# Softmax attention rebuilt: fp32r parts in two row tiles, wider exponentials, direct maxima

## The chip, the cores and the metric

The kernel runs on 1 core of one Trainium2 chip. The metric is the device time of one execution in microseconds. TensorE (PE) multiplies, VectorE (DVE), ScalarE (ACT) and GpSimd (POOL) work on elements, SyncE (SP) issues most DMAs. A difference of 0.2% is about what a measurement of this kernel can tell from none.

## What is computed

4096 tokens of 256 numbers pass a linear attention with exponential features, a layer norm, a transformer block, and a layer norm. The block is softmax attention with 16 heads of 16 numbers and a mixture of 8 experts, two per token. The part at issue, from the reference (the sequence is one batch of 4096):

```python
h = _layernorm(x, ln1_g, ln1_b)
q = (h @ Wq).reshape(Bb, Ss, H, Dh)
k = (h @ Wk).reshape(Bb, Ss, H, Dh)
v = (h @ Wv).reshape(Bb, Ss, H, Dh)
scores = jnp.einsum('bqhd,bkhd->bhqk', q, k) / jnp.sqrt(jnp.float32(Dh))
attn = jax.nn.softmax(scores, axis=-1)
ctx = jnp.einsum('bhqk,bkhd->bqhd', attn, v).reshape(Bb, Ss, Dd)
x = x + ctx @ Wo
```

Scores are large (Wq and Wk are scaled by 8), so q, k and the probabilities are carried in several parts of lower precision that add up to nearly fp32.

## The kernel before

The program runs its stages one after the other: linear attention with the projections (`linear_attention`), `softmax_attention`, `output_projection`, routing, dispatch, experts, combine.

In the last part of `linear_attention` each of eight chunks of 512 tokens is normalized (L407), transposed (L262), projected (L270, L276) and split into three bf16 parts: ScalarE writes the high one (L325), VectorE the rest (L423), ScalarE its middle (L331), VectorE the low one (L435). SyncE stores q, k and kd (the difference of the two halves of each 512 keys) to DRAM (L186, L190).

`softmax_attention` goes over 16 heads x 8 chunks of 512 queries; a chunk is a *step* of 16 units `t` of 256 keys (STEPS, STEP). Six products of parts stack up to 96 rows (SROWS); two more rows carry minus the maximum of each query (MROWS). In each unit TensorE does, in this order: `scores(t, 0)` (L683), `diff_unit` (L627), `scores(t, 1)`, `b_unit` (L636), `values` (L666) of five units ago (LAG). ScalarE turns scores into probabilities, two exponentials of 512 columns (L741), with the relu of `diff_unit` between them (L728). The maximum of each query over all keys is needed before the exponentials, so it is found seven steps ahead: for 1024 keys a unit computes b, the scores of one half, and diff, those of the other half minus b; max(b + relu(diff)) is made by one fused VectorE operation (`unit`, L797). diff_ps and b_ps have two buffers each. At the end of a step the tile maxima are reduced (L789), turned by TensorE (L642), split in two (L773, L775) and sent by SyncE into rows of q_ring (`rows`, L534). Probabilities are fp32; their upper 16 bits are read in place as bf16, and the low part is subtracted, by VectorE for 11 units (L804) and by GpSimd for 5 (L590). `values` multiplies both with V in three bf16 parts, as two column tiles side by side (partitions 0 to 63 and 64 to 127 of o_ps). Once a step ScalarE copies O (L733), TensorE turns it (L649), VectorE divides it (L781, L783) into ctx_slots. Before the first step stand seven steps of maxima only; in the last eight there are none.

The order on each engine is the order of the code; semaphores tie the engines together. `output_projection` gathers the heads (L880), turns them (L897), multiplies with Wo (L904) and adds x (L916) for each of eight chunks.

## Time and profile before

| | |
|---|---|
| median of 3 runs | 4858.36 us (4850.29 to 4861.54) |
| span of the profiled execution | 4852.0 us |
| PE, DVE, ACT, POOL busy | 4267.5, 3937.8, 3726.1, 2088.2 us |
| PE weight loads (overlap PE) | 1709.2 us |
| DMA | 176.11 MB, mean 36 GB/s |

The page's span goes from the first to the last instruction; it lies 6 us under the median. A busy share is an average over stages with different limits, so a change in one stage is read from that stage. Idle time of an engine is put down to the instruction that released it. TensorE's matmuls are pipelined: a row's duration reaches from its start to its last result, and the distance between two starts is what one costs in a stream.

### The profile page before, as it was taken

The page shows a single profiled execution, that of the slowest core. Times are in us where ns is not written, and L with a number is a line of the kernel's source. Part 1 is how long each engine was busy: PE and PEld are TensorE (multiplying, and loading weights), DVE is VectorE, ACT ScalarE, POOL GpSimd, SP SyncE. Part 2 cuts the span into 40 slices and gives each one's busy share as a digit, 9 for nine tenths or more (in the row PEclk, how much of TensorE's full clock was granted, in tenths as well). Part 3 has the DMA queues.
Part 4 walks back from the last instruction along what each step waited for, and adds up shares of the span by engine and source line. Part 5 has one row for each costly group of instructions (what it writes and reads, how often), then busy time and mean ns, then how long its engine had stood idle before and what let it go on. Part 6 is the DMA issues. An engine that isn't in the chain of part 4 may idle for free. (4 is left out here: it accounts for less than half of the span.)

```text
span 4852.0 us, 96386 instructions
## 1 busy us (share of the span) xinstructions
PE 4267.5 (88%) x22137; PEld 1709.2 (35%) x22137; DVE 3937.8 (81%) x7272; ACT 3726.1 (77%) x6966; POOL 2088.2 (43%) x1034
## 2 busy tenths in 40 slices
PE   7569999999999999999999999999999860899991
PEld 4322222222222222222222222222222350788881
DVE  3558898889899888989988898989998651788875
ACT  1347999999999999999999999999999720454440
POOL 0011343434444343434434343434434405787775
PEclk8777999999999999999999999999999965899995
DMA  2231010100101010100101010110100032333323
GB/s 77 100 81 17 0 17 0 17 6 11 17 0 17 0 17 0 17 11 6 16 0 17 0 17 0 17 16 0 17 0 1 37 104 88 134 122 121 124 98 112
DMA packets 105459, 176.11 MB, mean 36 GB/s; under 512 B 16512, under 2 KB 87552, under 8 KB 99072
## 3 DMA queue, kind: packets, MB, share of 16 engines
q1 hardware_dynamic: 86864, 146.17, 11.7%
q0 software_dynamic: 6336, 16.79, 1.1%
q10 hardware_dynamic: 12144, 12.06, 0.7%
q14 instruction: 97, 0.79, 0.1%
q8 instruction: 18, 0.29, 0.0%
HBM read 117.55 MB, written 57.15 MB: 36 GB/s over the span
## 5 line engine op out<-in xcount | busy, mean ns | idle before, releaser
L741 ACT ACTIVATE probs<-s_ps 128x512 f32<-128x512 f32 x4096 | 2427.4, 600 | 213.7 <-PE s_ps L683 160.9
L590 POOL TENSOR_TENSOR probs_low<-probs 128x1024 f16<-128x1024 f32 x640 | 1324.9, 2071 | 2082.7 <-ACT probs L741 2082.2
L804 DVE TENSOR_TENSOR probs_low<-probs 128x1024 f16<-128x1024 f32 x1408 | 1820.3, 1295 | 20.8 <-ACT probs L741 20.7
L797 DVE CUSTOM_DVE_ANT_0 excess<-b_ps,excess 128x512 f32<-128x512 f32 x2048 | 1402.1, 687 | 333.3 <-ACT excess L728 265.4
L683 PE MATMUL s_ps<-q_ring,k_ring 98*128 (+1 forms) x4096 | 1565.0, 384 | 14.4 <-ACT probs L741 9.3
L728 ACT ACTIVATE excess<-diff_ps 128x512 f32<-128x512 f32 x2048 | 1214.5, 593 | 58.2 <-PE diff_ps L627 48.2
L666 PE MATMUL o_ps<-probs,v_parts 128*64 128x512 bf16 x4106 | 853.9, 412 | 74.5 <-ACT o_here L733 72.2
L627 PE MATMUL diff_ps<-kd_ring,q_ring 96*128 (+1 forms) x2048 | 800.6, 391 | 50.8 <-issue 38.3
L683 PEld LDWEIGHTS s_ps<-q_ring,k_ring 98*128 98x128 bf16 x4096 | 434.8, 106 | 1159.8 <-ACT probs L741 572.4
L636 PE MATMUL b_ps<-k_ring,q_ring 96*128 (+1 forms) x2048 | 797.9, 390 | 12.5 <-DVE unit_max L797 11.9
L666 PE MATMUL o_ps<-probs_low,v_parts 128*64 128x512 f16 x4106 | 783.7, 378 | 0.0
L666 PEld LDWEIGHTS o_ps<-probs,v_parts 128*64 128x64 bf16 x4106 | 228.3, 106 | 907.8 <-issue 511.3
L1506 DVE TENSOR_TENSOR hidden_low<-hidden,hidden_high 128x512 fp32r<-128x512 f32 x184 | 436.6, 2397 | 123.1 <-ACT hidden_high L1470 122.8
L1466 ACT ACTIVATE hidden<-h_ps,b_here 128x512 f32<-128x512 f32 x184 | 127.1, 691 | 306.0 <-PE h_ps L1401 285.6
L1413 PE MATMUL y_ps<-w_high,hidden_high 128*128 128x256 f32 x736 | 213.4, 290 | 41.4 <-DVE hidden_low L1506 41.3
L636 PEld LDWEIGHTS b_ps<-k_ring,q_ring 96*128 (+1 forms) x2048 | 200.5, 98 | 128.2 <-DVE unit_max L797 61.3
L627 PEld LDWEIGHTS diff_ps<-kd_ring,q_ring 96*128 (+1 forms) x2048 | 201.4, 98 | 99.0 <-issue 93.1
L666 PEld LDWEIGHTS o_ps<-probs_low,v_parts 128*64 128x64 bf16 x4106 | 233.6, 109 | 0.3
L649 PEld LDWEIGHTS misc_ps<-gather,o_here 128*128 128x128 f32 x1032 | 153.2, 188 | 216.5 <-issue 215.3
L1413 PE MATMUL y_ps<-w_low,hidden_high 128*128 128x256 f32 x736 | 211.9, 288 | 0.0
L1413 PE MATMUL y_ps<-w_high,hidden_low 128*128 128x256 f32 x736 | 210.6, 286 | 0.0
L649 PE MATMUL misc_ps<-gather,o_here 128*128 128x17 f32 x1032 | 203.6, 273 | 0.7 <-ACT o_here L733 0.7
(199 smaller groups left out, 3521.3 us busy)
## 6 DMA issues: line engine op xcount, KB each, us to landing
w_in<-in_W SPq DMA_DIRECT2D x46, 1024.0 KB, 4.9
q_ring<-qs_dram SPq DMA_DIRECT2D x96, 128.0 KB, 4.4
k_ring<-ks_dram SPq DMA_DIRECT2D x96, 128.0 KB, 7.2
slots_dram<-zero_rows SPq DMA_DIRECT2D x24, 512.0 KB, 6.5
rows_e<-slots_dram SPq DMA_DIRECT2D x24, 512.0 KB, 3.9
y_slots_dram<-y_out ACTq DMA_DIRECT2D x23, 512.0 KB, 4.6
...
```

Source lines behind the costliest of these rows:

```text
L590: nc.gpsimd.tensor_tensor(probs_low[:, t % BUFS, :, :], probs[:, t % BUFS, :, :], high[:, :, :, 1], ALU.subtract).then_inc(pool_low_done, 1)
L627: nc.tensor.matmul(diff_ps[:, u % 2, :], q_ring[0:SROWS, ds(q, P)], kd_ring[:, ds(k, CHUNK)], start=True, stop=True).then_inc(diff_done, 1)
L636: nc.tensor.matmul(b_ps[:, u % 2, :], q_ring[0:SROWS, ds(q, P)], keys[:, :, 1, :], start=True, stop=True).then_inc(b_done, 1)
L649: last = nc.tensor.matmul(out_ps[:, t, :], o_here[:, P * t:P * t + P], gather[:, :], start=True, stop=True)
L666: last = nc.tensor.matmul(o_ps[V_COLS * k:V_COLS * k + V_COLS, :], v_parts[:, par, 2 * at + k, :], part[:, k, :], start=(t == 0 and low == ...
L683: nc.tensor.matmul(s2_ps[:, k, :], k_ring[:, col:col + P], q, start=True, stop=True).then_inc(s2_done, 1)
L728: nc.scalar.activation(excess[:, u % 2, :], diff_ps[:, u % 2, :], ACT.Relu).then_inc(excess_ready, 1)
L741: nc.scalar.activation(probs[:, t % BUFS, k, :], s2_ps[:, k, :], ACT.Exp).then_inc(exp_done, 1)
L797: nc.vector.tensor_tensor_reduce(excess[:, u % 2, :], b_ps[:, u % 2, :], excess[:, u % 2, :], 1.0, LEAST, ALU.add, ALU.max, unit_max[:, u ...
L804: nc.vector.tensor_tensor(probs_low[:, t % BUFS, :, :], probs[:, t % BUFS, :, :], high[:, :, :, 1], ALU.subtract).then_inc(low_done, 1)
L1413: last = nc.tensor.matmul(y_ps[:, b, t // 2, D * (t % 2):D * (t % 2) + D], h[:, f % 4, cols], w[:, b, f, :], start=(f == 0 and n == 0 and ...
L1506: nc.vector.tensor_tensor(hidden_low[:, f % 4, :], hidden[:, f % 2, :], hidden_high[:, f % 4, :].bitcast(F32), ALU.subtract).then_inc(low_ ...
```

## The change

Projections: q, k and kd are split into two fp32r parts instead of three bf16 ones, so ScalarE's middle parts and VectorE's low parts go. The stores are 8 a chunk instead of 6, of 8 bytes an element instead of 6.

Attention: three products of parts take 48 rows, so the scores of two key tiles are two row tiles, at partitions 0 and 64, and q is loaded to both places (q_stage, a chunk at a time, three ahead). One exponential takes both results, 1024 columns. The maximum is found two chunks ahead (LEAD) in 16 pairs of 512-column matmuls a chunk, in three banks of PSUM: in 11 pairs VectorE reduces both banks directly, in 5 (RELU_PAIRS) the old form with kd and a relu by ScalarE stays. The tile maxima are turned by VectorE in blocks of 32 and sent by 16 small DMAs. P times V: in 4 of 16 units (FULL_UNITS) P and V are multiplied in plain fp32, in 12 P is high and low as before; GpSimd makes the low parts of ten units, VectorE those of two, in four halves (DVE_PLACES). `values` come in ten visits, up to a slot in the next chunk (SLOTS). O is turned by one fp32 matmul of 512 columns (gather now 128 x 128), copied by ScalarE and stored undivided in DRAM with its sums. `output_projection` loads these, takes 1/z, spreads it over the heads with a matmul of ones, and VectorE multiplies; TensorE's transposes of heads and ScalarE's copies go, GpSimd adds x1 and x2. The division per chunk and ctx_slots go.

Longer functions are cut; lines taken away stand only where they are short.

```diff
-PARTS = 3
...
-Q_PARTS = (0, 0, 0, 1, 1, 2)
-K_PARTS = (0, 1, 2, 0, 1, 0)
...
+PARTS = 2
+Q_PARTS = (0, 0, 1)
+K_PARTS = (0, 1, 0)
...
+FULL_UNITS = (3, 7, 11, 15)
+DVE_UNITS = (2, 10)
+POOL_UNITS = (0, 1, 4, 5, 6, 8, 9, 12, 13, 14)
...
+DVE_PLACES = {5: (2, 0), 8: (2, 1), 11: (10, 0), 14: (10, 1)}
+VISITS = ((0, 1), (3,), (2, 4), (7,), (5, 6), (8, 9), (11,), (10, 12), (15,), (13, 14))
+SLOTS = (11, 12, 13, 14, 15, 16, 17, 18, 19, 21)
+COPY_SLOT, TURN_SLOT = 6, 8
+RELU_PAIRS = (2, 5, 8, 11, 14)
+FINISH_SLOTS = (4, 5, 6, 7)
+M_BANKS = tuple(((t + 1) % 3, t % 3 if t < UNITS - 1 else 2) for t in range(UNITS))
...
-                for s in range(5):
-                    act.wait_ge(rest_ready, c * 5 + (s + 6))
-                    nc.scalar.activation(parts[:, b, s, 1, :], rest[:, s, :], ACT.Copy).then_inc(mid_ready, 1)
...
-                for s in range(5):
-                    dve.wait_ge(mid_ready, c * 5 + (s + 1))
-                    nc.vector.tensor_tensor(parts[:, b, s, 2, :], rest[:, s, :], parts[:, b, s, 1, :], ALU.subtract
-                                            ).then_inc(low_ready, 1)
...
+        s_ps = ps("s_ps", [P, 2, 2, CHUNK])
+        m_ps = ps("m_ps", [P, 3, CHUNK])
...
+            def rows(n, buf):
+                sp.wait_ge(max_ready, n + 1)
+                for at in (0, TOP_ROW):
+                    for r in range(MROWS):
+                        row = q_stage[at + SROWS + r:at + SROWS + r + 1, ds(buf * CHUNK, CHUNK)].bitcast(F32)
+                        row = row.rearrange("a (t b n) -> a t b n", t=TPC, b=P // SQ)
+                        for b in range(P // SQ):
+                            sp.dma_start(row[:, :, b, :], max_turned[SQ * b:SQ * b + TPC, r, :]).then_inc(rows_in, 16)
...
+                for t in POOL_UNITS:
+                    pool.wait_ge(exp_done, i * UNITS + (t + 1))
+                    nc.gpsimd.tensor_tensor(probs_low[:, LOW_UNITS.index(t), :, :], probs[:, t, :, :],
+                                            high_view[:, t, :, :, 1], ALU.subtract).then_inc(pool_low_done, 1)
...
+            def max_pair(it, c, t):
+                g = it * (PAIR * UNITS) + (c * UNITS + t)
+                par, buf = c % PAIR // CHUNKS, c % Q_BUFS
+                col = buf * CHUNK + P * (t // KCH)
+                key = CHUNK * (t % KCH)
+                relu = t in RELU_PAIRS
+                keys = kd_ring[0:SROWS, par, key:key + CHUNK] if relu else k_ring[0:SROWS, par, key:key + CHUNK]
+                sides = [(keys, 0, M_BANKS[t][0]), (k_ring[TOP_ROW:TOP_ROW + SROWS, par, key:key + CHUNK], TOP_ROW, M_BANKS[t][1])]
                 if t == 0:
+                    sides.reverse()
+                for n, (keys, at, bank) in enumerate(sides):
+                    if c * UNITS + t > 1 - n:
+                        pe.wait_ge(m_read, g - 1 + n)
+                    last = nc.tensor.matmul(m_ps[:, bank, :], q_stage[at:at + SROWS, col:col + P], keys,
+                                            start=True, stop=True)
+                last.then_inc(m_done, 1)
+            def scores(it, c, t):
+                par, buf = c % PAIR // CHUNKS, c % Q_BUFS
+                if c * UNITS + t > 1:
+                    pe.wait_ge(exp_done, it * (PAIR * UNITS) + (c * UNITS + t - 1))
+                for k, at in enumerate((0, TOP_ROW)):
+                    last = nc.tensor.matmul(s_ps[:, t % 2, k, :], k_ring[at:at + AROWS, par, P * t:P * t + P],
+                                            q_stage[at:at + AROWS, buf * CHUNK:buf * CHUNK + CHUNK], start=True, stop=True)
+                last.then_inc(s_done, 1)
+            def values(it, c, visit):
...
+                for t in VISITS[visit]:
+                    if t in POOL_UNITS:
+                        pe.wait_ge(pool_low_done, i * len(POOL_UNITS) + (POOL_UNITS.index(t) + 1))
+                    if t in DVE_UNITS:
+                        pe.wait_ge(dve_low_done, i * (2 * len(DVE_UNITS)) + 2 * (DVE_UNITS.index(t) + 1))
...
+                    if t in FULL_UNITS:
+                        for k in range(2):
+                            last = nc.tensor.matmul(o_ps[V_COLS * k:V_COLS * k + V_COLS, :],
+                                                    v_full[:, par, FULL_UNITS.index(t), k, :], probs[:, t, k, :],
+                                                    start=False, stop=False)
+                        continue
+                    for n, part in enumerate((high_view[:, t, :, :, 1], probs_low[:, LOW_UNITS.index(t), :, :])):
+                        for k in range(2):
+                            last = nc.tensor.matmul(o_ps[V_COLS * k:V_COLS * k + V_COLS, :],
+                                                    v_parts[:, par, first_tile(t) + 2 * k, :], part[:, k, :],
+                                                    start=(first and n == 0), stop=(final and n == 1))
                 last.then_inc(pv_done, 1)
...
+            def turn_o(it, c):
+                pe.wait_ge(o_copied, it * PAIR + c)
+                nc.tensor.matmul(o_ps[:, :], gather[:, :], o_here[:, :], start=True, stop=True).then_inc(o_turned, 1)
+            def chunk(it, c, ahead):
+                it = pe.snap(it) if ahead and c > 0 else it
                 if ahead:
+                    load_waits(it, c + LEAD)
+                pe.wait_ge(rows_in, (it * PAIR + (c + 1)) * ROW_DMAS)
+                for t in range(UNITS):
+                    scores(it, c, t)
                     if ahead:
+                        max_pair(it, c + LEAD, t)
+                    for visit, slot in enumerate(SLOTS):
+                        if slot == t:
+                            values(it, c, visit)
+                        if slot == t + UNITS and c > 0:
+                            values(it, c - 1, visit)
+                    if t == TURN_SLOT and c > 0:
+                        turn_o(it, c)
...
+            def excess_pair(n, t):
+                act.wait_ge(m_done, n * UNITS + (t + 1))
+                nc.scalar.activation(excess[:, :], m_ps[:, M_BANKS[t][0], :], ACT.Relu).then_inc(excess_ready, 1)
...
+            def chunk(i, b, ahead, first=False, later=None):
+                for t in range(UNITS):
+                    act.wait_ge(s_done, i * UNITS + (t + 1))
+                    if not first:
+                        act.wait_ge(pv_done, i * len(VISITS) + (visit_of(t) + 1 - len(VISITS)))
+                    nc.scalar.activation(probs[:, t, :, :], s_ps[:, t % 2, :, :], ACT.Exp).then_inc(exp_done, 1)
+                    if t == COPY_SLOT and not first:
+                        copy_o(i)
+                    if t == TURN_SLOT and not first:
+                        copy_ctx(i, 1 - b, later)
+                    if ahead and t in RELU_PAIRS:
+                        excess_pair(i + LEAD, t)
...
+            def pair(n, t, b):
+                qt, j = t // KCH, t % KCH
+                if t in RELU_PAIRS:
+                    dve.wait_ge(excess_ready, n * len(RELU_PAIRS) + (RELU_PAIRS.index(t) + 1))
+                    dve.sem_inc(dve_passed, 1)
+                    nc.vector.tensor_tensor_reduce(excess[:, :], m_ps[:, M_BANKS[t][1], :], excess[:, :], 1.0, LEAST,
+                                                   ALU.add, ALU.max, unit_max[:, b, qt, 2 * j:2 * j + 1]
+                                                   ).then_inc(m_read, 1)
+                else:
+                    dve.wait_ge(m_done, n * UNITS + (t + 1))
+                    lo = min(M_BANKS[t])
+                    nc.vector.tensor_reduce(unit_max[:, b, qt, 2 * j:2 * j + 2], m_ps[:, lo:lo + 2, :],
+                                            AX.X, ALU.max).then_inc(m_read, 1)
+            def finish_max(n, b, step):
...
+            def low(i, t, k):
+                dve.wait_ge(exp_done, i * UNITS + (t + 1))
+                nc.vector.tensor_tensor(probs_low[:, LOW_UNITS.index(t), k, :], probs[:, t, k, :], high_view[:, t, k, :, 1],
+                                        ALU.subtract).then_inc(dve_low_done, 1)
+            def chunk(n, b, ahead=True, current=True, finish=True):
+                for t in range(UNITS):
                     if ahead:
+                        pair(n, t, b)
+                    if current and t in DVE_PLACES:
+                        low(n - LEAD, *DVE_PLACES[t])
+                    if finish and t in FINISH_SLOTS:
+                        finish_max(n - 1, 1 - b, FINISH_SLOTS.index(t))
...
+                for j in range(HALVES):
+                    heads = of_head[:, c, HEADS // 2 * j:HEADS // 2 * j + HEADS // 2, :].rearrange("p h d -> p (h d)")
+                    last = nc.tensor.matmul(z_ps[:, c % 2, j, :], heads, z_inv[:, :], start=True, stop=True)
+                last.then_inc(z_spread, 1)
...
+                    nc.vector.tensor_tensor(headsT[:, c % 2, j, :], ctxT[:, c, j, :], z_ps[:, c % 2, j, :], ALU.mult
+                                            ).then_inc(headsT_ready, 1)
```

## Rows read from the trace of the kernel before

**Rows 1.** Page part 1: busy us (share of the span), instructions.

```profile
PE 4267.5 (88%) x22137; PEld 1709.2 (35%) x22137; DVE 3937.8 (81%) x7272; ACT 3726.1 (77%) x6966; POOL 2088.2 (43%) x1034
```

**Rows 2.** Busy us by stage: stretch, length, PE, PEld, DVE, ACT, POOL; PE clock.

```profile
322.40:426.30 103.90, 92.22 (x233) 23.92 (x233) 79.81 (x243) 66.59 (x112) 0.00 (x0) 0.65 0.00 0
426.30:3710.70 3284.40, 3183.29 (x16581) 936.68 (x16579) 2945.85 (x5809) 3093.13 (x5930) 1374.30 (x674) 1.00 0.07 9
3710.70:3863.10 152.40, 143.60 (x762) 44.86 (x761) 126.05 (x117) 125.47 (x232) 77.12 (x36) 1.00 0.00 0
3863.10:3929.00 65.90, 40.15 (x192) 33.46 (x192) 37.43 (x76) 20.62 (x50) 0.33 (x1) 0.84 0.17 68
```

**Rows 3.** Page part 5, ScalarE: busy us, mean ns, idle before.

```profile
L741 ACT ACTIVATE probs<-s_ps 128x512 f32<-128x512 f32 x4096 | 2427.4, 600 | 213.7 <-PE s_ps L683 160.9
...
L728 ACT ACTIVATE excess<-diff_ps 128x512 f32<-128x512 f32 x2048 | 1214.5, 593 | 58.2 <-PE diff_ps L627 48.2
```

**Rows 4.** Timeline in mid attention: start us, duration us, engine, line, operation.

```profile
2000.48 1.22 DVE L804 TENSOR_TENSOR probs_low<-probs 128x1024 f16<-128x1024 f32 x1
...
2000.75 2.70 POOL L590 TENSOR_TENSOR probs_low<-probs 128x1024 f16<-128x1024 f32 x1 [2.50 <-ACT probs L741]
...
2001.23 0.38 PE L636 MATMUL b_ps<-k_ring,q_ring 96*128 x1
...
2001.54 0.41 PE L666 MATMUL o_ps<-probs,v_parts 128*64 128x512 bf16 x2
...
2002.10 0.39 PE L683 MATMUL s_ps<-q_ring,k_ring 98*128 x1
```

**Rows 5.** Groups of instructions by line: wider copy, and reductions of two widths.

```profile
L1454 ACT ACTIVATE m_high<-mT_e 128x1024 fp32r<-128x1024 f32 x24 | 25.4, 1057 | 0.8
...
L1058 DVE TENSOR_REDUCE top_logit<-logits 128x32 f32<-128x256 f32 x1 | 0.4, 420 | 12.5 <-ACT logits L1007 12.5
...
L789 DVE TENSOR_REDUCE tile_max<-unit_max 128x4 f32<-128x16 f32 x135 | 22.9, 169 | 17.1 <-issue 12.1 <-DVEq L764 0.8
```

**Rows 6.** Timeline of the maxima made ahead, at low and high clock.

```profile
395.84 0.63 PE L636 MATMUL b_ps<-k_ring,q_ring 96*128 x1
...
410.14 0.08 DVE L797 DVE_READ_ACCUMULATOR2_ANT unit_max<- 128x1 f32 x1
...
410.28 0.39 PE L636 MATMUL b_ps<-k_ring,q_ring 96*128 x1 [0.36 <-DVE unit_max L797]
...
410.31 0.60 ACT L728 ACTIVATE excess<-diff_ps 128x512 f32<-128x512 f32 x1 [0.37 <-DVE unit_max L797]
...
411.10 0.69 DVE L797 CUSTOM_DVE_ANT_0 excess<-b_ps,excess 128x512 f32<-128x512 f32 x1 [0.26 <-ACT excess L728]
```

**Rows 7.** Low parts by line: duration ns min/median/max, first and last start.

```profile
L804 DVE TENSOR_TENSOR probs_low<-probs x1408: 1209/1221/2548, 429.1 to 3857.3; 128x1024 f16<-128x1024 f32 x176
...
L1506 DVE TENSOR_TENSOR hidden_low<-hidden,hidden_high x184: 676/2200/5094, 4136.6 to 4741.9; 128x512 fp32r<-128x512 f32 x184
...
L590 POOL TENSOR_TENSOR probs_low<-probs x640: 1893/1896/2874, 434.9 to 3857.9; 128x1024 f16<-128x1024 f32 x160
```

**Rows 8.** Timeline of the experts' stage: fp32r matmuls in a stream and after waiting.

```profile
4235.01 0.39 PE L1413 MATMUL y_ps<-w_high,hidden_high 128*128 128x256 f32 x1 [1.88 <-DVE hidden_low L1506]
...
4300.06 0.39 PE L1401 MATMUL h_ps<-m_low,w_high 128*128 128x512 f32 x1
...
4300.29 0.39 PE L1401 MATMUL h_ps<-m_high,w_low 128*128 128x512 f32 x1
...
4300.72 0.69 ACT L1466 ACTIVATE hidden<-h_ps,b_here 128x512 f32<-128x512 f32 x1 [1.47 <-PE h_ps L1401]
```

**Rows 9.** Timeline: transposes in the projections, Wo matmuls in the output projection.

```profile
275.82 1.20 PE L262 MATMUL banks<-ident,hn 128*128 128x128 f32 x8 [3.50 <-DVE hn L407]
...
3884.50 3.72 PE L904 MATMUL banks_o<-w_o,headsT 128*128 128x256 f32 x16 [1.18 <-ACT headsT L886]
```

**Rows 10.** Timeline at attention's start: six loads of q issued by SyncE.

```profile
299.97 3.01 SPq L520 DMA_DIRECT2D q_ring<-qs_dram  x6
```

667 lines of the change are left out of this document (298 added, 369 removed).

## The prediction

> **What bounds the kernel now.** I read the page's busy shares first [rows 1]: TensorE is busy 88% of the span, VectorE 81%, ScalarE 77%. They average over stages, so the busy time by stage comes next [rows 2]. Softmax attention from its first matmul to its last takes 103.9 + 3284.4 + 152.4 = 3540.7 of 4852.0 us, and the change is there. In the long stretch 120 chunks (one head by 512 queries) take 27.4 us each, 1.71 us per slot (a sixteenth of a chunk). ScalarE is busy 3093 of those 3284 us, TensorE 3183. Per slot ScalarE does two exponentials and a relu of 512 columns each [rows 3]. TensorE is only just behind: in [rows 4] it goes from b (2001.23) over the two pairs of values matmuls to the next scores (2002.10), one 512-column stream per 0.22 to 0.31 us, without idling. GpSimd is busy 1374 us of it and has slack. So a slot is priced by throughput: buffers are double and waits are short.
>
> **The change, part by part.** *Engine sums per chunk.* ScalarE: 16 exponentials of 1024 columns. A 1024-column copy took 1.06 us [rows 5], a 512-column exponential 0.60 [rows 3]; between them I take 1.03, so 16.5, plus five relus and two copies at 0.59: 20.6 us. VectorE: 11 reductions of 1024 columns, which the trace has only small: 0.42 us for 256 columns, 0.17 for 16 [rows 5], that is 1.05 ns per column, 1.22 us for 1024. Five fused relu-add-maxima at 0.69 [rows 6], four halves of low parts at 0.6 (half of the 1.22 in [rows 7]), small ones 0.7: some 20 us. GpSimd: ten low parts at 1.90 [rows 7], 19 us. TensorE: fp32r streams 512 columns per 0.23 us, about as bf16 does (4300.06, then 4300.29) [rows 8]. Two row tiles side by side have no row here; bounds are 0.23 and 0.46 us for the scores of a slot. I take 0.25, because the two column tiles of a values pair in [rows 4] do run together (both within 0.41). 16 scores 4, 32 maximum matmuls 7.4, values 8 (a plain fp32 unit is two passes of one pair, which is as long as high and low part), some 20 changes of tiling at 0.1 (b to values 0.31 instead of 0.22), the turn of O 0.5: 22 us. All four sums lie under today's 27.4. By them alone the change would win.
>
> *The wait that takes their place.* m_ps has three banks and a maximum pair uses two. Pair t takes banks (t+1)%3 and t%3, and the latter is one that pair t-1 also used. So the second matmul of every pair waits for m_read of the pair before, and VectorE's reduction waits for that matmul. The pieces add up in a circle. Reduction 1.22. VectorE's end to the matmul's start 0.06 (410.22 to 410.28) [rows 6]. The matmul: an fp32r one of 256 columns that came after a wait took 0.39 [rows 8]; 256 columns more at 2.4 GHz are 0.11, so 0.50. Its end to the reader's start 0.04 (4300.68 to 4300.72) [rows 8]. Together 1.82 us. In the five relu slots ScalarE is put in: 0.06 + 0.50 + 0.04 + relu 0.60 + 0.19 until VectorE starts (410.91 to 411.10) + 0.69 [rows 6] = 2.08. A chunk is 11 x 1.82 + 5 x 2.08 = 30.4 us. This is the term that decides: VectorE stands idle for 0.6 us in each pair although no engine is full. Today's pair of double buffers (diff_ps and b_ps each have two) has no such circle. Queued behind the waiting matmul on TensorE are the values of its slot and the next scores, and ScalarE waits for those.
>
> *What comes on top.* I walked one chunk slot by slot with these prices. (a) Slot 8: the turn of O stands behind the maximum pair on TensorE, and ScalarE copies it before the relu of slot 8: 0.5 us of fp32 passes plus 0.6 of copy on the circle, +1.1. (b) In slots 2 and 14 the relu stands behind an exponential whose scores came after the values of the slot before: +0.9 for both. (c) The low halves sit behind relu pairs, where the 0.6 us of waiting covers them; but those of slots 5 and 14 start while GpSimd has begun a unit. In [rows 4] a GpSimd operation that starts during VectorE's lasts 2.70 instead of 1.90 us, so one waits for the other; +1.2 for both, bounds 0 and 4 x 1.9. (d) Visits of two low units fill TensorE for 2.0 us where the circle has 1.82: +0.2. Sum 33.8. (e) The clock. In the stretch from 322.4 to 426.3 TensorE did only maximum matmuls with waits between and was granted 0.65 of full speed on average [rows 2], so 1.2 GHz for some 70% of it. Slots 6 to 10 of a new chunk are such work, with scores added. A matmul on the circle is then 0.24 longer (395.84: 0.63 against the 0.39 of 410.28) [rows 6]; over five slots at 70% plus the slower turn that is +1.1; bounds 0 and, if slots with values were hit too, +4. A chunk is 34.9 us.
>
> *Low parts and the port.* The low halves are the one place where VectorE reads two SBUF operands beside GpSimd. In the experts' stage, where GpSimd is never idle, such an operation took a median of 2200 ns against 676 at least; in attention the median is 1221 and the least 1209 [rows 7]. The Trainium skill, SBUF — State Buffer, "Who interferes with whom", says that the later of the two is fully blocked, and that a reduction never contends. By that rule each of the four low halves could cost one whole GpSimd unit; the experts' rows agree, the attention rows nearly never show it, since there the starts rarely meet.
>
> *Stages.* Ahead work: 2 chunks instead of 7, at the low clock: 2 x (11 x 2.06 + 5 x 2.32) = 69 us for 103.9. Then 126 x 34.9 = 4397. The last two chunks have no maximum and go by GpSimd's 19, 40 together. Draining the last chunk, with a turn, a copy and a store, 8. Total 4514 for 3540.7: +973. Projections before attention: ScalarE's five mid copies and VectorE's five low subtractions go, but TensorE's next chunk waited for hn, made ahead of these [rows 9], so 0, bounds -3 and +3 for the larger stores. SyncE: six loads take 3.01 us to issue [rows 10], so 16 small row transfers take 8 and land some 10 us after the maximum of slot 7; nine slots (18 us) cover them, with 6 loads issued earlier in the chunk. With cover of under 10 us a chunk would start late; at a chunk of 34.9 it isn't. Loading at the start (27 transfers behind a larger memset) comes out like today's. Output projection: a 16-matmul group took 3.72 us [rows 9], the spread of 1/z adds 1.0, so 4.8 instead of 5.8 a chunk, and a somewhat earlier start: -14. The sum is 4852 + 973 - 14 = 5811 us of the profiled span; the median stands 6 us above the span, so 5817.
>
> **The rivals.** *Faster.* The round trip is hidden after all and the fullest engine bounds, with a tenth of friction: 24.5 us a chunk. 69 + 126 x 24.5 + 48 = 3204, so 4507 us. It decides at a chunk of 27.3 us, where both kernels meet. For it: four balanced sums. Against: the bank order leaves no pair in advance, and 1.22 + 0.06 + 0.39 is already 1.67 without any exposed load. 7%. *A shorter circle.* No exposed weight load (0.39 for 0.50), half of the extras, full clock: 31 us, 69 + 126 x 31 + 48 = 4023, so 5326 us. 20%. *Tiles one after the other.* If row tiles, or fp32 column tiles, don't overlap, TensorE has up to 27.6 us, and slots with values run over the circle by 0.2 to 0.5: 38.5 us, so 6270. 10%. *Low clock throughout.* TensorE's 22 us become some 40 with the waits in it: 40 us, so 6460. 10%. *The port lock as a rule.* Each of four low halves waits 1.9: 7.6 for 1.2, 41.3 us, so 6620. 5%. It is what the Trainium skill's SBUF page, named above, would make of these halves at its worst.
>
> **How the numbers follow.** My own case (33 to 37 us a chunk, 5580 to 6080) has 48% and gives the time: 5817. The cases of over 5330 and under 6250 come to 80%: outside are the faster case (7), the lock (5), half of the low-clock case (5) and the end of the short circle (3). A difference of 0.2%, 10 us, is what a measurement can tell from none; no case ends there but by chance: faster 0.07, same 0.01, slower 0.92.
>
> **What would show it.** Right: VectorE's maximum reduction lasts 1.22 us, with some 0.6 idle ahead of each, ended by the maximum matmul; that matmul waits for VectorE; all engines under 70% busy in attention; chunks of 33 to 37 us; a granted clock under 1 in places. Wrong: reductions back to back; scores 0.46 apart; a reduction much under 1.2 us; low halves of over 2 us; idle time of ScalarE ended by row transfers. The forecast falls if the pair of a slot is in PSUM before VectorE has finished the one before.

## The result, and the profile after

The changed kernel takes 6591.9 us (median of 4 runs, 6579.3 to 6602.8), the kernel before 4854.3 us beside it: a ratio of 1.3577 with a 95% interval of 1.3552 to 1.3602. The forecast was slower, 5817 us, in a range of 5330 to 6250. The side was right and the time is 775 us beyond it. I forecast 959 us of loss (5811 less 4852, both spans) and got 1738.

The profiled execution spans 6584.6 us. First the busy shares of the page of after (they answer to [rows 1]), then its busiest groups: line, engine, operation, count, busy us, mean ns, idle us before and what ended it.

```profile
PE 4863.7 (74%) x21172; PEld 2180.0 (33%) x21172; DVE 3704.8 (56%) x4769; ACT 2934.9 (45%) x3557; POOL 3263.2 (50%) x1749
...
L767 ACT ACTIVATE probs<-s_ps 128x1024 f32<-128x1024 f32 x2048 | 2080.7, 1023 | 2261.1 <-PE s_ps L675 2260.8
L666 PE MATMUL m_ps<-k_ring,q_stage 48*128 48x512 f32 x3456 | 1600.2, 550 | 1279.2 <-DVE unit_max L807 987.2
L807 DVE TENSOR_REDUCE unit_max<-m_ps 128x2 f32<-128x1024 f32 x1408 | 1720.5, 1222 | 895.4 <-PE m_ps L666 895.4
...
L801 DVE CUSTOM_DVE_ANT_0 excess<-m_ps,excess 128x512 f32<-128x512 f32 x640 | 442.3, 691 | 1430.0 <-ACT excess L750 1430.0
```

No engine is full any more: ScalarE fell from 77% to 45%, and sits idle for as long as it works on exponentials. VectorE's reduction is 1222 ns, as worked out; the second matmul of a pair waits for the reduction of the pair before, and the next reduction waits for that matmul.

By stage (stretch, length, busy us of PE, PEld, DVE, ACT, POOL, granted clock, then DMA), which answers to [rows 2]: ahead work, 126 chunks, the last two, the output projection.

```profile
320.00:388.00 68.00, 25.91 (x63) 9.58 (x63) 33.09 (x45) 5.97 (x10) 2.20 (x2) 0.50 0.00 0
388.00:5567.00 5179.00, 3951.16 (x16357) 1463.89 (x16357) 2907.21 (x3656) 2491.80 (x2897) 2567.92 (x1386) 0.76 0.05 10
5567.00:5613.00 46.00, 40.65 (x222) 14.06 (x220) 14.13 (x11) 33.42 (x38) 39.73 (x20) 1.00 0.01 2
5613.00:5672.00 59.00, 43.46 (x160) 31.05 (x160) 37.15 (x91) 5.61 (x12) 21.30 (x11) 0.89 0.45 153
```

Attention takes 5293 us where it took 3540.7. Three stages came out as forecast: 68 for 69, 46 for 48, and everything behind attention is 17 us shorter where 14 were said. The whole miss is in the long stretch: 5179 / 126 = 41.1 us a chunk for 34.9.

The timeline of one chunk's middle, slots 5 to 8 (start us, duration, engine, line, operation; in brackets the idle time before and its releaser):

```profile
2986.14 6.05 POOL L620 TENSOR_TENSOR probs_low<-probs 128x1024 f16<-128x1024 f32 x3 [4.42 <-ACT probs L767]
...
2988.62 1.82 DVE L831 TENSOR_TENSOR probs_low<-probs 128x512 f16<-128x512 f32 x1
...
2990.36 1.85 DVE L817 TENSOR_SCALAR max_parts<-tile_max 128x4 fp32r<-128x4 f32 x1
2992.12 1.21 DVE L807 TENSOR_REDUCE unit_max<-m_ps 128x2 f32<-128x1024 f32 x1
...
2993.39 0.79 PE L666 MATMUL m_ps<-k_ring,q_stage 48*128 48x512 f32 x1 [3.90 <-DVE unit_max L807]
...
2996.22 2.07 PE L708 MATMUL o_ps<-o_here,gather 128*128 128x512 f32 x2
...
2998.41 0.59 ACT L760 ACTIVATE ctx_stage<-o_ps 17x512 f32<-17x512 f32 x1 [2.66 <-PE o_ps L708]
...
2998.91 0.57 ACT L750 ACTIVATE excess<-m_ps 128x512 f32<-128x512 f32 x1
...
2999.66 0.69 DVE L801 CUSTOM_DVE_ANT_0 excess<-m_ps,excess 128x512 f32<-128x512 f32 x1 [4.06 <-ACT excess L750]
```

Read it downwards. GpSimd has a run of three subtractions, until 2992.19. VectorE's low half of 512 columns takes 1.82 us (0.65 is the shortest one in this trace), and then a multiplication of four columns takes 1.85 and ends where GpSimd's run ends. Only then comes the reduction for which TensorE has waited 3.90 us. TensorE comes back at half its clock (0.79 for the 0.50 of such a matmul at full clock), turns O in 2.07 us, and the copy, the relu and the maximum of slot 8 stand behind that, one after the other.

The clock over two chunks:

```profile
2969.20:2993.10 23.90, 18.03 (x97) 7.03 (x95) 15.33 (x18) 13.11 (x15) 15.09 (x8) 1.00 0.04 9
2993.10:3010.20 17.10, 13.18 (x35) 4.41 (x35) 7.96 (x13) 6.66 (x8) 5.21 (x3) 0.50 0.02 3
3010.20:3034.10 23.90, 17.74 (x99) 7.11 (x97) 15.48 (x18) 13.11 (x15) 14.41 (x8) 1.00 0.38 58
3034.10:3054.60 20.50, 16.96 (x51) 5.83 (x51) 8.88 (x12) 7.69 (x10) 7.94 (x4) 0.50 0.01 3
```

TensorE runs 23.9 us at 2.4 GHz and then 17 to 20 at 1.2. From 600 to 4800 us, 102 chunks, the clock falls 108 times; in nine of ten cases it falls in slot 7 or 8 of the table below, around the pause, and comes back in slot 13 or 14. The forecast had half clock in five slots and priced it at 1.1 us.

### The profile page after: what moved, and what is told of

Its sections match the earlier page's. It is cut to its first block and busy times, and to the rows that moved or that the text cites. A ratio compares the mean times of both kernels' runs of the same rounds, so it can differ in the third digit from the quotient of the medians.

```text
span 6584.6 us, 74964 instructions
## 1 busy us (share of the span) xinstructions
PE 4863.7 (74%) x21172; PEld 2180.0 (33%) x21172; DVE 3704.8 (56%) x4769; ACT 2934.9 (45%) x3557; POOL 3263.2 (50%) x1749
## 3 DMA queue, kind: packets, MB, share of 16 engines
q8 instruction: 163, 2.67, 0.2%
## 5 line engine op out<-in xcount | busy, mean ns | idle before, releaser
L620 POOL TENSOR_TENSOR probs_low<-probs 128x1024 f16<-128x1024 f32 x1280 | 2513.6, 1976 | 2674.8 <-ACT probs L767 2669.1
L767 ACT ACTIVATE probs<-s_ps 128x1024 f32<-128x1024 f32 x2048 | 2080.7, 1023 | 2261.1 <-PE s_ps L675 2260.8
L666 PE MATMUL m_ps<-k_ring,q_stage 48*128 48x512 f32 x3456 | 1600.2, 550 | 1279.2 <-DVE unit_max L807 987.2
L807 DVE TENSOR_REDUCE unit_max<-m_ps 128x2 f32<-128x1024 f32 x1408 | 1720.5, 1222 | 895.4 <-PE m_ps L666 895.4
L675 PE MATMUL s_ps<-q_stage,k_ring 50*128 50x512 f32 x4096 | 1437.2, 578 | 20.1 <-issue 16.3
L666 PEld LDWEIGHTS m_ps<-k_ring,q_stage 48*128 48x128 f32 x3456 | 702.1, 232 | 2026.1 <-DVE unit_max L807 1449.3
L801 DVE CUSTOM_DVE_ANT_0 excess<-m_ps,excess 128x512 f32<-128x512 f32 x640 | 442.3, 691 | 1430.0 <-ACT excess L750 1430.0
L675 PEld LDWEIGHTS s_ps<-q_stage,k_ring 50*128 50x128 f32 x4096 | 555.7, 224 | 1101.9 <-issue 746.2
L694 PE MATMUL o_ps<-probs,v_full 128*64 128x512 f32 x2048 | 651.6, 720 | 0.0
L831 DVE TENSOR_TENSOR probs_low<-probs 128x512 f16<-128x512 f32 x512 | 584.3, 1142 | 22.6 <-ACT probs L767 22.6
```

The lines of the kernel that those rows point to most:

```text
L620: nc.gpsimd.tensor_tensor(probs_low[:, LOW_UNITS.index(t), :, :], probs[:, t, :, :], high_view[:, t, :, :, 1], ALU.subtract).then_inc(pool ...
L666: last = nc.tensor.matmul(m_ps[:, bank, :], q_stage[at:at + SROWS, col:col + P], keys, start=True, stop=True)
L675: last = nc.tensor.matmul(s_ps[:, t % 2, k, :], k_ring[at:at + AROWS, par, P * t:P * t + P], q_stage[at:at + AROWS, buf * CHUNK:buf * CHUN ...
L694: last = nc.tensor.matmul(o_ps[V_COLS * k:V_COLS * k + V_COLS, :], v_full[:, par, FULL_UNITS.index(t), k, :], probs[:, t, k, :], start=Fal ...
L767: nc.scalar.activation(probs[:, t, :, :], s_ps[:, t % 2, :, :], ACT.Exp).then_inc(exp_done, 1)
L801: nc.vector.tensor_tensor_reduce(excess[:, :], m_ps[:, M_BANKS[t][1], :], excess[:, :], 1.0, LEAST, ALU.add, ALU.max, unit_max[:, b, qt, 2 ...
```

## The experiments

I held three theories of the missing 6.2 us a chunk: VectorE's collision with GpSimd and what piles up behind it in slots 5 to 9; the low clock; the fp32 passes on TensorE. Slot lengths below are distances between the starts of ScalarE's exponentials t-1 and t, means over 120 chunks, worked out from all of them in each trace. So the turn of O, which stands behind the scores and maxima of slot 8 in TensorE's queue, lengthens slot 9 of the table, and the low half and the multiplication of four columns, which VectorE has behind pair 5, lengthen slot 8. The expectations of the first runs, up to e5_pool, count by the starts of VectorE's maxima instead; there the same two stalls are slot 6 (4.12 us) and slot 8 (5.40 us). "Clock" is the granted clock from 600 to 4200 us, which lies inside attention in every kernel, and "half" the time per chunk at 1.2 GHz that follows from it (2 x (1 - clock) x chunk, before rounding).

| kernel | median us | chunk | clock | half | slots 6+7 | 8 | 9 | 10 | 11+12 | 13+14 |
|---|---|---|---|---|---|---|---|---|---|---|
| after | 6591.9 | 41.1 | 0.76 | 19.4 | 4.10 | 4.66 | 4.62 | 2.36 | 6.29 | 4.84 |
| e1_bank | 6145.6 | 37.8 | 0.79 | 15.9 | 3.42 | 4.64 | 3.95 | 2.45 | 4.47 | 4.49 |
| e2_port | 6310.3 | 38.9 | 0.79 | 16.2 | 4.10 | 2.66 | 4.75 | 2.37 | 6.29 | 4.44 |
| e3_warm | 6452.4 | 39.8 | 0.83 | 13.2 | 4.67 | 4.29 | 3.83 | 2.56 | 5.21 | 4.19 |
| e4_turn9 | 6380.4 | 39.4 | 0.78 | 17.3 | 4.10 | 4.66 | 2.10 | 4.68 | 5.03 | 4.61 |
| e5_pool | 6165.2 | 37.7 | 0.79 | 15.6 | 4.10 | 1.99 | 4.48 | 2.41 | 6.29 | 4.73 |
| e7_high | 6629.0 | 41.6 | 0.58 | 34.8 | 5.56 | 1.54 | 5.10 | 2.37 | 6.29 | 5.11 |
| e8_nowarm | 5475.7 | 32.3 | 0.86 | 9.1 | 3.42 | 0.90 | 1.40 | 4.46 | 4.02 | 4.51 |
| e6_all | 5522.3 | 32.7 | 0.97 | 1.9 | 4.12 | 1.12 | 2.65 | 3.18 | 3.06 | 4.19 |
| e9_fill7 | 6591.1 | 41.1 | 0.78 | 18.4 | 5.71 | 2.81 | 4.56 | 2.37 | 6.29 | 5.11 |
| e10_fill78 | 5577.5 | 33.2 | 0.88 | 8.1 | 4.08 | 1.16 | 1.40 | 4.23 | 3.94 | 4.76 |
| e11_high8 | 5501.0 | 32.6 | 0.76 | 15.6 | 3.85 | 0.92 | 1.77 | 4.52 | 4.14 | 3.97 |
| e12_noport | 6171.1 | 37.7 | 0.79 | 15.9 | 4.10 | 1.38 | 5.07 | 2.41 | 6.29 | 4.79 |
| e13_noport2 | 6169.5 | 37.7 | 0.77 | 17.3 | 4.10 | 1.37 | 4.71 | 2.37 | 6.29 | 5.15 |
| e14_best | 5445.9 | 32.2 | 0.87 | 8.5 | 3.42 | 0.90 | 1.39 | 4.47 | 3.95 | 4.43 |

**The circle.** Every maximum matmul gets the next of the three banks and is reduced by itself:

```diff
-M_BANKS = tuple(((t + 1) % 3, t % 3 if t < UNITS - 1 else 2) for t in range(UNITS))
+M_BANKS = tuple((2 * t % 3, (2 * t + 1) % 3) for t in range(UNITS))
...
-                    nc.vector.tensor_reduce(unit_max[:, b, qt, 2 * j:2 * j + 2], m_ps[:, lo:lo + 2, :],
-                                            AX.X, ALU.max).then_inc(m_read, 1)
+                    for side in range(2):
+                        dve.wait_ge(m_done, n * (2 * UNITS) + (2 * t + side + 1))
+                        nc.vector.tensor_reduce(..., m_ps[:, M_BANKS[t][side], :], AX.X, ALU.max).then_inc(m_read, 1)
...
```

> Each of the 32 maximum matmuls of a chunk writes the next of the three banks, signals by itself and is reduced by itself (512 columns), so that a bank comes free before VectorE has read the pair; VectorE gets 11 more instructions a chunk, and nothing is left out. Theory of the circle (the step that the forecast gave most of its time to): the 1.81 us of a plain slot is the reduction of 1.22 us plus a matmul that waits for it; two reductions of some 0.61 us with their starts hide the matmul, a plain slot falls to 1.35 to 1.5 us, and with some eight plain slots in a chunk the chunk loses 2.5 to 3.5 us: 126 times that is 300 to 450 us off the 6592, to 6150 to 6300. Theory of the stalls and the clock (the excess over the forecast is in slots 6 and 8 and in the stretch at half clock, not in the circle): the slots without low halves and turns fall, but the long ones stay at 4.1 and 5.4 us and TensorE, idle for longer between them, is at half clock for a larger part; the gain is under 150 us. If VectorE's own fixed cost of an instruction outweighs it, the time is 6592 or more.

6145.6 us, 446 us less: the circle's own forecast, 126 x 3.3 us. But the gain isn't where I put it. Slots 2 and 3, plain ones with a values visit ahead, only went from 1.92 to 1.81 and from 1.80 to 1.68 us; there TensorE is busy all the time anyway (no idle time in after's slots 2 and 3). The 3.3 us are in slots without a visit (slot 6: 2.70 to 2.02) and in slots 9, 11 and 12, at half clock. So the circle is real, and bounds the slots in which TensorE has idle time left.

**The port, first way.** The four-column multiplication becomes a reduction:

```diff
-nc.vector.tensor_scalar(max_parts[:, 0, 0:TPC], tile_max[:, :], -1.0, None, ALU.mult).then_inc(high_done, 1)
+nc.vector.tensor_reduce(max_parts[:, 0, 0:TPC], unit_max[:, b, :, :], AX.X, ALU.max, negate=True).then_inc(high_done, 1)
```

> The negated tile maximum is taken by a second reduction of unit_max with a sign change (128 x 32 to 4 columns) in place of the multiplication of 4 columns by -1; same numbers, same place. Theory of the shared port: the 4-column multiplication took 1853 ns in the median because GpSimd's subtraction held the port, a reduction of about the same size (its neighbour, the tile maximum) takes 145 ns, so slot 6 falls from 4.12 us to about 2.4 and 126 chunks lose 1.7 us each: 215 us, to about 6375; somewhat more if the shorter idle time of TensorE there keeps the clock up. Rival, what the multiplication waited for isn't the port but its operand: the reduction in its place is as long and nothing changes, 6592 within 20. Rival, the next instruction on VectorE takes over the wait (the low part of the maximum, in the next slot): the gain is under 60 us.

6310.3 us, 282 less. The instruction's durations (min/median/max ns) in after and here:

```profile
L817 DVE TENSOR_SCALAR max_parts<-tile_max x128: 156/1853/1860, 368.1 to 5571.5; 128x4 fp32r<-128x4 f32 x128
```

```profile
L817 DVE TENSOR_REDUCE max_parts<-unit_max x128: 171/173/181, 367.8 to 5286.6; 128x4 fp32r<-128x32 f32 x128
```

In the same place, with the same four results, one takes 1853 ns and the other 173. It wasn't the data that it waited for. The Trainium skill, SBUF — State Buffer, "Who interferes with whom", has this: an instruction of VectorE in a two-port mode (it names tensor_scalar) and one of GpSimd block each other for a whole instruction, one with two SBUF inputs contends with a GpSimd instruction that reads SBUF, and a reduction never contends on trn2. The two rows agree. Slot 8 lost 2.0 us.

**Filling TensorE's idle time.** Here the scores matmuls of six slots are repeated into the same banks:

```diff
-                for k, at in enumerate((0, TOP_ROW)):
+                for k, at in enumerate((0, TOP_ROW) * (4 if t in (4, 6, 7, 8, 9, 10) else 1)):
+                    k = k % 2
```

> The scores matmuls of slots 4, 6, 7, 8, 9 and 10 are written four times over into the same banks, with the same result; nothing else changes. It adds 36 matmuls of 512 columns a chunk to TensorE, some 0.25 us each at full clock as two row tiles side by side or 0.5 a pair when not, in slots where TensorE stands idle. Theory of the clock: TensorE is at 1.2 GHz for 17 to 20 us of every 41 because it stands idle around slots 6 and 8; with that time filled the granted clock stays above 0.95, plain slots of 2.10 us fall to 1.82, slot 8 from 5.4 to about 4, slots 11 to 14 to 2.1 to 2.5: 3 to 5 us of a chunk, 380 to 630 us off the 6592. Theory that the clock is a consequence and costs nothing (the waits on VectorE and GpSimd set the slots): no change, or up to 3 us a chunk more for the added matmuls on the path, 6592 to 6970.

6452.4 us, 140 less where 380 to 630 were expected, with 36 matmuls more in a chunk. The clock rose to 0.83 and not over 0.95. Slots 4 and 6 grew by 0.68 and 0.57 where the repeats lay on the path, and slots 8 to 15 gave back 2.7. So work at half clock seems to cost time, but filling pauses is a poor way to avoid it. Of the 2.7, slot 8's 0.37 may be no more than time that slots 6 and 7 took over, as in e9_fill7 below.

**The turn of O.**

```diff
-COPY_SLOT, TURN_SLOT = 6, 8
+COPY_SLOT, TURN_SLOT = 6, 9
```

> The turn of O (a matmul in fp32, ScalarE's copy of the result) stands in slot 9 instead of slot 8, where ScalarE also has a relu and VectorE a low half; the copy of O before it stays in slot 6. Theory of the pile (slot 8 is 5.4 us because turn, copy, relu and the low half stand one behind the other): slots 8 and 9 together fall from 6.9 us by the 0.6 us of the copy ahead of the relu and part of the turn's 2.1 us, 1 to 2 us a chunk, 125 to 250 us off the 6592. Rival (the turn takes its 2.1 us on TensorE wherever it stands): slot 9 grows by what slot 8 loses, 6592 within 40.

6380.4 us, 212 less. Slots 9 and 10 together nearly stay (6.98 to 6.78): the turn takes its time wherever it stands, as the rival said, though the rival wanted no gain. The other 1.5 us went in slots 11 to 14, where less was left at half clock, and slot 9 became a plain circle slot at half clock, 2.10. Size right, place wrong.

**VectorE's low halves go to GpSimd.**

```diff
-DVE_UNITS = (2, 10)
-POOL_UNITS = (0, 1, 4, 5, 6, 8, 9, 12, 13, 14)
+DVE_UNITS = ()
+POOL_UNITS = (0, 1, 2, 4, 5, 6, 8, 9, 10, 12, 13, 14)
...
-DVE_PLACES = {5: (2, 0), 8: (2, 1), 11: (10, 0), 14: (10, 1)}
+DVE_PLACES = {}
...
+                    if not (isinstance(n, int) and n == 0):
+                        dve.wait_ge(rows_in, n * ROW_DMAS)
```

> Units 2 and 10, whose low halves VectorE took in four pieces of 512 columns, go to GpSimd, which then subtracts 12 units of 1024 a chunk; VectorE has no low halves (its transposition waits for the rows of the maximum by itself, which the low halves did for it). Theory that VectorE's low halves block its maxima while GpSimd subtracts (1227 ns in the median, 2379 at most, against 650 undisturbed): 4.6 us of VectorE a chunk go, of which slots 6 and 8 give back some 2 us and slots 12 and 15 some 0.5: 250 to 320 us off the 6592. Rival, the four-column multiplication in slot 6 then waits by itself for GpSimd's unit and takes most of it back: under 120 us. Rival, GpSimd's added 3.8 us (two units of 1.9) make units 10 and 12 late for their visits: 6592 or more.

6165.2 us, 427 less, above the highest expectation. The multiplication behind it still waited (1290 ns in the median), yet slot 8 lost 2.67 us: with no low half ahead of it, it waits for an earlier subtraction of GpSimd's run. Slot 1 lost 0.56.

**The fp32 units.** The four fp32 units are multiplied by their high parts in one pass, so the low part of P is left out for them:

```diff
-                                                    v_full[:, par, FULL_UNITS.index(t), k, :], probs[:, t, k, :],
+                                                    v_parts[:, par, first_tile(t) + 2 * k, :], high_view[:, t, k, :, 1],
```

> The four units in fp32 (3, 7, 11, 15) are multiplied by their high parts in one bf16 pass instead of the fp32 product, so the low part of P is left out for them: each costs TensorE 0.23 us instead of 1.0 at full clock, 3.1 us less of TensorE a chunk. It is an upper bound for what the fp32 product costs against the two 16 bit passes (0.5 us). Theory that the fp32 unit is a term of the chunk (it stands in slots 12, 14, 1 and 3, ahead of the next scores in TensorE's queue): 1.5 to 3 us a chunk, 190 to 380 us off the 6592. Rival, those slots are set by VectorE's circle and the relu, and less work on TensorE only lowers the clock for longer: 6592 within 60.

6629.0 us: not faster, but 37 slower, with 3.1 us of TensorE's work gone from each chunk (four units of 1.0 us at full clock that now take 0.23). This is the stretch from 600 to 4800 us of after, and the same of this kernel:

```profile
600.00:4800.00 4200.00, 3205.67 (x13269) 1186.63 (x13269) 2353.56 (x2960) 2018.58 (x2348) 2091.57 (x1138) 0.76 0.05 10
```

```profile
600.00:4800.00 4200.00, 3533.99 (x12331) 1341.24 (x12331) 2184.60 (x2933) 2010.71 (x2325) 2028.76 (x1129) 0.58 0.05 10
```

Fewer matmuls, more busy time, clock 0.58. Slot 13 shows the price of the fp32 unit (2.74 to 1.72); slots 0 and 6 went from 2.79 and 2.70 to 4.21 and 4.16. And slot 8 lost 3.1 us, since with other starts the four-column multiplication mostly missed GpSimd's run:

```profile
L817 DVE TENSOR_SCALAR max_parts<-tile_max x128: 155/156/1861, 365.6 to 5623.3; 128x4 fp32r<-128x4 f32 x128
```

So two savings, up to 3.1 us of TensorE's work and some 2.3 of the kind that e2_port brought, stand against 15.4 us more at half clock, and the sum is 0.4 us longer. That the clock took both back is the reading that fits; no run holds the clock and takes the units out.

**Four edits together**, and the same with the fill:

> Four edits together: a bank for every maximum matmul, the reduction in place of the 4-column multiplication, the turn of O in slot 9, VectorE's low halves on GpSimd. Alone the first three gave 447, 282 and 211 us. If the causes are separate terms of the chunk, the sum of them and some 200 for the last is 1140 and the time some 5450 (43.3 - 9 is some 32 us a chunk). If they share the same stall (around slots 6 to 8), the sum of the gains is 70% of that: 5790. If the clock, with fewer pauses, comes back to full for most of the chunk, the stretch gains another 2 us a chunk: 5200.

5475.7 us, 1116 less than after; alone the four gave 446, 282, 212 and 427, 1366 in all before rounding, so 82% of the sum. A chunk is 32.3 us.

> The same four edits and the scores matmuls of slots 4 and 6 to 10 written four times over. If the clock is still at half for a good part of the chunk without them, they give another 100 to 250 us as they did alone (140). If the four edits already keep it up, the added matmuls (36 a chunk, 0.25 us a pair and more) stand on TensorE's path and cost 0 to 2 us a chunk, 0 to 250 us over the kernel without them. For this kernel to reach the 4847 of before, the chunk would have to fall to 27.3 us; none of the theories says so.

5522.3 us. The clock went to 0.97 and nothing was won. Between these two kernels the slots can be compared at both clocks: slots 10 to 14 are 12.99 us without the fill and 10.43 with it, the turn of O alone 2.07 and 1.12:

```profile
3000.36 2.07 PE L717 MATMUL o_ps<-o_here,gather 128*128 128x512 f32 x2
```

```profile
2981.07 1.12 PE L718 MATMUL o_ps<-o_here,gather 128*128 128x512 f32 x2
```

That is 2.56 us for 7.2 us less at half clock, 0.36 us for each. The repeats in slots 4, 6, 8 and 9 cost 2.87. By this rate, an estimate, the 19.4 us at half clock in after cost about 7 us a chunk, and 1.1 were forecast.

The chunks within one kernel say much the same without an edit. In e6_all 88 of 120 chunks ran at full clock from end to end and took 31.9 us in the mean; the other 32 had 7.2 us at half and took 34.9. In after no chunk is free of half clock, but its length rises by 0.36 us for each us at half (a line through 120 chunks, correlation 0.6). A longer chunk has also more room for half clock, so this is a correlation and not a proof; no run has after at full clock.

**A fill in the pause alone, and on the better kernel.** First the scores of slot 7 eight times in after, then those of slots 7 and 8 four times in the kernel with the four edits:

```diff
+                for k, at in enumerate((0, TOP_ROW) * (8 if t in (7,) else 1)):
```

> The kernel after with one edit: the scores matmuls of slot 7 are written eight times over, seven of them extra. They stand where TensorE waits 3.9 us for VectorE in the trace (2989.5 to 2993.4 us), 0.33 us a pair at full clock, 2.3 us in all, so that they lie in idle time, where the repeats of slots 4 and 6 lay on the path. Theory that the pause ahead of slot 8 brings the clock down and the low clock costs time: the granted clock rises from 0.76 to over 0.85 and slots 8 to 14 give back 2 to 4 us a chunk, 250 to 500 us off the 6592, more than the 140 of the wider fill. Rival, the clock falls wherever the pause ends, and the filled part only shortens it: clock under 0.80, gain under 80 us. Rival, the clock rises and the time stays, since other waits set the slots: 6592 within 60.

6591.1 us, nothing. The eight pairs took 2.32 us and the pause that followed was still 2.29, so it lost 1.6 of its 3.9 us; slot 7 grew by 1.6 and slot 8 lost 1.85. The clock rose from 0.76 to 0.78 only. The rival said this.

> The kernel with the four edits (5475 us) and the scores matmuls of slots 7 and 8 written four times over, 12 matmuls more a chunk, where TensorE waits for VectorE before the turn of O. Theory of the clock: it is at 0.84 there and falls in slots 8 to 12 only; with the fill it stays up, the turn takes 1.0 instead of 2.07 us and slots 10 and 12 lose 1.3 and 1.0 us as they did with the wider fill (4.46 to 3.18 and 3.10 to 2.14), without its price in slots 4, 6 and 9 (0.7, 0.7 and 1.25 us): some 2 us a chunk, 5475 - 250 = 5225. Rival, the added work makes the scores of slot 9 late by as much: 5475 within 60.

5577.5 us, 102 slower than without: clock 0.88 for 0.86, slot 10 at 4.23 us, the turn mostly still at half clock (1061 ns a record in the median, as without). But this run didn't fill the pause that it aimed at. Without the repeats TensorE had no idle time in slot 8 and 0.3 us in slot 7; they made these slots 0.26 and 0.66 us longer, and the pause that TensorE has in slot 10 grew from 1.1 to 1.9 us. In 34 of 120 chunks the clock was full throughout, and these took 30.4 us where the others took 34.3. The theory's expectations of the time failed in both runs; only the wide fill of e6_all held the clock, and what is enough to hold it I can't say from these runs.

**The fp32 units once more**, on the kernel with the four edits (low part of P left out for them again):

> The kernel with the four edits (5475 us) and the four fp32 units multiplied by their high parts alone in one bf16 pass (the low part of P is left out for them): TensorE has 3.1 us less a chunk at full clock. In the kernel after, the same edit left the time and brought the granted clock from 0.77 to 0.63. Theory that the fp32 units are on the path and the clock undid their removal: here too the clock falls below 0.75 and the time changes by less than 150 us either way. Rival, with the pauses of slots 5 to 8 gone the clock keeps up and the fp32 units show their price: 1.5 to 3 us a chunk, 190 to 380 us off the 5475.

5501.0 us for 5475.7, with runs that overlap (5485 to 5523, and 5455 to 5502), so no gain rather than a loss; clock 0.76 for 0.86. Slots 2, 4 and 13 lost 0.6, 0.9 and 0.95, slot 14 and slots 0, 1 and 6 gained 0.4, 0.75, 0.69 and 0.43. As before, less work for TensorE went with a lower clock and left the time.

**What pins slots 8 and 9.** Both port edits together, and nothing else:

> The kernel after with the two edits that take VectorE's four-column multiplication and its low halves out of GpSimd's way, and nothing else: the circle of three banks and the turn of O in slot 8 stay. Alone they gave 282 and 427 us. The forecast of 34.9 us a chunk held 1.2 us for this collision. Theory that the collision is the term that was mis-sized: the two pieces of slot 8 are different waits and add up to 620 to 700 us, 5.0 to 5.6 us a chunk, 35.5 to 36.1 us a chunk and 5890 to 5970 us, which leaves 1.8 to 2.4 us above the forecast without its own 1.2 for the low clock and the fp32 units. Rival, both remove the same stall: 6100 to 6165. Rival, with the stall gone the clock comes back too: under 5800.

6171.1 us, the same as the low halves' removal alone (6165.2). The rival (both remove the same stall, 6100 to 6165) was right, and the trace shows what followed: VectorE's next small instruction, the low part of the maximum, took over the wait. First the GpSimd run and that instruction in e5_pool, then in e12_noport:

```profile
2964.86 5.60 POOL L620 TENSOR_TENSOR probs_low<-probs 128x1024 f16<-128x1024 f32 x3 [2.46 <-ACT probs L767]
...
2969.68 0.80 DVE L820 SCALAR_TENSOR_TENSOR max_parts<-tile_max,max_parts 128x4 fp32r<-128x4 f32 x1
```

```profile
2963.60 5.60 POOL L620 TENSOR_TENSOR probs_low<-probs 128x1024 f16<-128x1024 f32 x3 [2.45 <-ACT probs L767]
...
2967.90 1.31 DVE L820 SCALAR_TENSOR_TENSOR max_parts<-tile_max,max_parts 128x4 fp32r<-128x4 f32 x1
```

2964.86 + 5.60 is 2970.46, and the instruction ends at 2970.48; 2963.60 + 5.60 is 2969.20, and it ends at 2969.21. In after it takes 145 ns. So the third instruction went off the port too:

```diff
-                    nc.vector.scalar_tensor_tensor(max_parts[:, 1, 0:TPC], tile_max[:, :], -1.0, ...)
+                        nc.vector.tensor_reduce(max_parts[:, 1, 0:TPC], tile_max[:, :, :], AX.X, ALU.add, negate=True)
```

> As the run before it (no low halves on VectorE, a reduction in place of the 4-column multiplication; 6171 us, 37.7 us a chunk), and the low part of the maximum is taken by a reduction too (the negated sum of the maximum and its negated high part, with one more reduction to lay the high part beside it), so that nothing small on VectorE needs GpSimd's port; same numbers. Theory of the pinned slot (whatever small instruction comes last waits for the end of GpSimd's subtractions, 1315 ns in the run before): slots 8 and 9, 6.45 us together, lose 1.2 us: 150 us off, 6020. Rival, the turn of O and its low clock set slot 9: 6171 within 40. Rival, GpSimd's subtractions wait in turn for VectorE and lengthen: more than 6171.

6169.5 us. The instruction now takes 152 ns, slot 9 lost 0.36 us against e12_noport, and the chunk stays at 37.7: slots 0, 13 and 14 took it back. Here the clock changes in e5_pool and in e13_noport2, one period of each:

```profile
2948.40:2972.20 23.80, 19.13 (x105) 7.62 (x101) 14.49 (x19) 14.14 (x16) 17.27 (x10) 1.00 0.04 9
2972.20:2985.80 13.60, 10.84 (x30) 3.44 (x30) 5.07 (x7) 5.64 (x7) 6.09 (x4) 0.50 0.02 3
```

```profile
2947.40:2967.60 20.20, 16.81 (x95) 6.71 (x89) 10.99 (x18) 12.34 (x16) 14.74 (x8) 1.00 0.04 11
2967.60:2984.80 17.20, 13.64 (x39) 4.65 (x41) 6.43 (x10) 7.38 (x9) 7.81 (x5) 0.50 0.01 3
```

37.4 us each time, but 3.6 us more of it at half clock in these two periods; in the mean of all chunks it is 1.7 more than in e5_pool and 1.4 more than in e12_noport. At 0.36 us for each, 1.4 is 0.5 us, about what slot 9 gave. My theory of the pinned slot was right for the run before and fell for this one. That the low clock now holds the chunk fits these numbers and isn't shown by them.

> The four edits together (5475 us, 32.3 us a chunk) and the low part of the maximum by a reduction. There it took 256 ns in the median and 1824 at most. Theory: at most 0.3 us a chunk are to be had, 5440 to 5475. If the one more reduction of 0.18 us a chunk stands on VectorE's path instead, 5475 to 5500. None of the theories brings it near the 4858 of the kernel before: what remains is the turn of O (4.5 us in slot 10) and slots 0, 4, 12 and 13 of 2.6 to 3.1 us, where TensorE is the last to be ready.

5445.9 us (5439.8 to 5485.3), the lowest median of these variants, though its runs overlap with the four edits alone (5455 to 5502), and 1.126 times the kernel before (1.121 to 1.131). Slot 10 with the turn takes 4.47 us, slots 0, 4, 12 and 13 take 2.6 to 3.0. I found no version of the changed kernel that reaches the one before.

## Why the prediction was wrong in size, step by step

The circle gives 30.4 us a chunk and stands. I added 4.5 us for what comes on top, (a) to (e), and 10.7 were measured. The steps that failed are the sizes of three of these terms: the collision (c) at 1.2 us, where removing the low halves gave 3.4; the clock (e) at 1.1, where the estimate above says some 7; and the turn (a) at 1.1, where moving it gave 1.7. Of the two rivals nearest to the time, neither happened as told: the low clock throughout (6460) had TensorE at half all the time, where the granted clock was 0.76, and the lock (6620) is answered under (c).

- **Engine sums under 27.4 us don't decide; the circle does.** Right. The circle's pieces came out to the hundredth (1222 ns, idle 0.58 before it, 0.50 the matmul), 1.80 to 1.82 us in plain slots at full clock. Breaking it gave 446 us. Where a values visit fills the slot, TensorE alone needs 0.33 for the scores, 0.33 for the maxima and 1.0 for the values, nearly as long, which I hadn't seen.
- **(c), 1.2 us for the low halves beside GpSimd.** Mis-sized, and its list was incomplete. I called the low halves "the one place" where VectorE meets GpSimd and put all small instructions at 0.7 us. The four-column multiplication takes 1853 ns in the median and stands right behind a blocked low half. Removing the low halves gave 3.4 us a chunk, against 1.2 forecast for them; taking the multiplication off the port alone gave 2.3, and both together again 3.3 (e12_noport), so it is one stall. I also read the experts' stage as one in which GpSimd is never idle; it is busy for 461 of 605 us there. The rival of the lock gave 6620 us for 6592, but with another make-up (four low halves at 1.9 each; their median is 1227), so its nearness is mostly chance.
- **(a), the turn of O, 1.1 us.** Mis-sized. I took 0.5 us for its fp32 passes. The fp32 matmul of 512 columns (two records in the trace) takes 1.12 us at full clock and 2.07 at half, and slot 9, which carries it, 4.62 us where a plain slot has 1.82. Moving it gave 1.7 us.
- **(e), the clock, 1.1 us with a bound of +4.** By the estimate this is the largest miss. I saw half clock in the maxima made ahead and carried it to slots 6 to 10; it lasts 19.4 us of a chunk in the mean, through the values of slots 11 to 13. The rate from e6_all and e8_nowarm makes it some 7 us. The step that failed is that I priced the clock by five slots, 0.24 us of one matmul in each and a slower turn, and not as a loop: at half clock slots 11 and 12 are longer too (6.29 us together, 3.06 in e6_all at 0.97, with the four edits in), and the chunk with them. The clock falls about where TensorE pauses for 3.8 us in slot 8, and less of that stall (e5_pool) went with less time at half (19.4 to 15.6); what exactly brings it down stays open.
- **fp32 units at 0.5 us.** Wrong by a factor of two. In the trace of after (line 694) such a unit holds TensorE from 2983.49 to the next scores at 2984.50, 1.0 us, where high and low parts take 0.46 (four starts from 2987.11 to 2987.80, 0.23 apart). The Trainium skill, FP8 and Floating Point Precision, "TensorE Precision Notes", gives an fp32 matmul four passes through the array; the trace agrees, since 1.0 us is four times the 0.23 to 0.25 of a stream, and I had counted two, which no run shows. It cost no time that I could show: without it the clock fell.
- **(b) and (d), 0.9 and 0.2 us.** Not separated. VectorE's maxima start 4.51 us apart over slots 2 and 3 and 5.08 over slots 14 and 15 (medians), where the circle has 3.90: 1.8 in all, with the fp32 units of slots 14, 1 and 3 in it (slots by VectorE's maxima here).
- **Scores as row tiles side by side.** Right: the two of a pair start 3 ns apart (2979.996 and 2979.999), and the next matmul follows 0.33 us after them (2981.81 to 2982.14).
- **Stages.** 68 for 69, 46 for 48, -17 for -14. The 16 row transfers take 9.85 us to issue for the 8 worked out, and no engine's idle time is ended by them.
- **The signs.** The reduction's 1.22 us, the idle time ahead of it and the matmul that waits for VectorE are as named. Two signs of being right failed: a chunk of 33 to 37 us (41.1), and every engine under 70% busy in attention (TensorE is at 3951 of 5179 us, 76%, a good part of it at half clock).

The terms overlap, and so don't add up to the 6.2 us between 34.9 and 41.1: the collision makes the pause, about there the clock falls, and at half clock the turn is twice as long. The four edits give 10.7 us a chunk one by one, and 8.8 together.
